# Image units by matrix products under the LSTM: five per image instead of three, with a third PSUM bank

## The reference, cut to what matters

```python
x = x + halo_attention(_gn(x))            # 8x8 blocks, windows of 14x14, 4 heads
x = x + lstm_over_columns(_gn(x))         # 96 time steps, hidden size 128, then a linear layer
x = x + deformable_conv(_gn(x))           # below
x = x + _L3_conv_ref(_gn(x), L3_conv_M)   # an 8x8 block transform on both sides
```

```python
offset = conv2d(x, p_w, p_b, 1, 1)
m = jax.nn.sigmoid(conv2d(x, m_w, m_b, 1, 1))
...
x_off = g_lt[:, None] * gather(qx_lt, qy_lt) + g_rb[:, None] * gather(qx_rb, qy_rb) + g_lb[:, None] * gather(qx_lt, qy_rb) + g_rt[:, None] * gather(qx_rb, qy_lt)
x_off = x_off * jnp.transpose(m, (0, 2, 3, 1))[:, None]
...
return conv2d(x_off, conv_w, None, stride=KS, padding=0)
```

## Time and profile before

| | |
|---|---|
| median of 3 runs | 3619.52 us |
| the profiled execution: time, span | 3624.01 us, 3622.2 us |
| first gather on POOL starts | 519.1 us |
| attention(1), lstm(1), prepare(1) begin | 563.6, 870.7, 1222.9 us |
| attention(2), lstm(2), prepare(2) begin | 1315.1, 1624.6, 1981.7 us |
| attention(3), lstm(3), prepare(3) begin | 2085.3, 2406.3, 2766.8 us |
| transform(0) begins, sampling after transform(1) begins | 2881.1, 2947.1 us |
| last gather starts, transform(3) begins | 3589.65, 3600.6 us |

### The profile page before, as it was taken

One profiled execution on the slowest core, in us unless ns is written; L12 is line 12 of the kernel. 1 busy time (PEld: TensorE's weight loads), 2 busy tenths in 40 slices (PEclk: granted clock), 3 DMA queues, 4 the chain that ended last, 5 costly groups with the idle time before them and its releaser, 6 DMA issues. The chain is left out here.

```text
span 3622.2 us, 59607 instructions
## 1 busy us (share of the span) xinstructions
PE 2785.3 (77%) x21833; PEld 2027.9 (56%) x21833; DVE 2479.2 (68%) x5480; ACT 1263.4 (35%) x3105; POOL 2380.0 (66%) x2445
## 2 busy tenths in 40 slices
PE   6979984885899748867998568668987376889882
PEld 4667763664676526646666346546665254555542
DVE  4754447985777669965777679756777675677763
ACT  4644433542433315523333145324333121222210
POOL 3200026777777777777777777777777777777774
PEclk9999996886899868876999779768999688999995
DMA  6622025764321346636212376543213432222211
GB/s 214 194 60 73 1 71 166 208 174 93 88 60 53 106 145 192 193 82 123 59 53 68 96 216 193 145 94 87 59 54 104 87 94 73 65 63 70 59 53 48
DMA packets 270803, 374.53 MB, mean 103 GB/s; under 512 B 109508, under 2 KB 181336, under 8 KB 269992
## 3 DMA queue, kind: packets, MB, share of 16 engines
q1 hardware_dynamic: 166688, 200.21, 19.2%
q0 software_dynamic: 76896, 157.64, 16.0%
q10 hardware_dynamic: 26928, 12.87, 1.6%
HBM read 270.08 MB, written 99.55 MB: 102 GB/s over the span
## 5 line engine op out<-in xcount | busy, mean ns | idle before, releaser
L769 POOL DMA_INDIRECT got<-sample_table,index x2403 | 2325.2, 968 | 1092.3 <-issue 726.6
L1618 PE MATMUL gates<-cells,row_hat 128*128 128x400 f32 x1782 | 653.3, 513 | 67.8 <-DVE spanned L1153 53.2
L1618 PEld LDWEIGHTS gates<-cells,row_hat 128*128 128x128 f32 x1782 | 332.7, 194 | 309.6 <-issue 84.2
L1175 DVE TENSOR_TENSOR got<-got,bank 128x864 f32<-128x864 f32 x267 | 279.6, 1047 | 242.5 <-DMA got<-sample_table,index 234.3
L852 ACT ACTIVATE pt<-gates 98x512 f32<-98x512 f32 x528 | 288.6, 594 | 325.8 <-PE gates L1726 304.7
L1826 PEld LDWEIGHTS gates<-hist,whh 128*128 128x128 f32 x2280 | 313.5, 205 | 138.7 <-DVE hist L1469 100.8
L1826 PE MATMUL gates<-hist,whh 128*128 128x96 f32 x2280 | 325.9, 290 | 53.8 <-DVE hist L1469 53.1
L1286 DVE TENSOR_REDUCE mx<-gates 128x2 f32<-128x392 f32 x576 | 295.5, 553 | 82.3 <-PE gates L1712 80.9
L1606 PE MATMUL bank<-turned,wout 128*128 128x96 f32 x1728 | 244.9, 304 | 131.5 <-DVE turned L1203 66.1
L1606 PEld LDWEIGHTS bank<-turned,wout 128*128 128x128 f32 x1728 | 239.0, 219 | 156.4 <-DVE turned L1203 110.5
L1712 PE MATMUL gates<-kst,qst 96*128 96x196 bf16 x1152 | 185.2, 278 | 119.7 <-DVE mx L1286 103.1
(11 more groups left out here) (188 smaller groups left out, 4791.6 us busy)
## 6 DMA issues: line engine op xcount, KB each, us to landing
kst<-k_parts SPq DMA_DIRECT2D x96, 441.0 KB
got<-sample_table,index POOLq DMA_INDIRECT x2403
qst<-q_parts SPq DMA_DIRECT2D x96, 288.0 KB
k_parts<-kp SPq DMA_DIRECT2D x24, 882.0 KB
k_parts<-kp SPq DMA_DIRECT2D x24, 588.0 KB
q_parts<-qp SPq DMA_DIRECT2D x24, 576.0 KB
spread<-locations ACTq DMA_DIRECT2D x84, 144.0 KB, 3.9
sample_table<-tab SPq DMA_DIRECT2D x12, 784.0 KB
```

What stands on the lines that cost most here:

```text
L769: pool.indirect_dma_start(out=got[:, g % RING, n, :], out_offset=None, in_=tables[p], in_offset=bass.IndirectOffsetOnAxis(ap=at, axis=0)). ...
L1175: dve.tensor_tensor(corners, corners, w[:, :, 0:3].unsqueeze(3).to_broadcast([P, NTAP, 3, C]), ALU.mult).then_inc(weighted, 1)
L1618: mm = pe.matmul(sums_of(s, h), row_hat[:, 3 * v % HATS + n // TAPS3, t, n % TAPS3, :], cells[:, t, C // 2 * h:C // 2 * (h + 1), :].rearra ...
```

## The change

Five units of each of images 0, 1, 2 (62 to 66) are made by products under the next LSTM instead of three (60 to 62): 45 steps or 270 products in each of lstm(1) to lstm(3), before 27 steps or 162. 27 units are then made by products, and 261 gathered (2349 gathers, before 2403). Nothing changes in which units of image 3 are made by products.

The products start at time step 12 instead of 14 and are spread to step 94. Their sums rotate through three PSUM banks (3, 4, 6). To free bank 3, the output gate moves into bank 1 beside the tanh gate; PE therefore waits in every step for the tanh activation (`g_act`) before the output gate's recurrent product, and the output gate's inputs come first. DVE calls its point ahead of its dense sums, and reads a half in the step in which PE makes it instead of the next. The row positions of the units are turned by one transpose of 36 rows for each unit, copied from up to three banks, and stored by one DMA. `SAMPLES` buffers and `located` share `dense_work`.

The units of each stage change: attention 26, 25, 26 (before 28, 28, 29), with 7, 4, 5 of them in its first six points; LSTM 34, 34, 34 (31, 31, 32); `prepare` 12, 12, 12 (9, 11, 11), of which 7 are gathered (6, 8, 8). 215 units are done by the end of prepare(3), before 210, and 216 by that of transform(1) in both.

```diff
-        stages += [(6 + 3 * NU, ATTENDED[p]), (W, STEPPED[p]), (prep_points(p), PREPARED[p])]
+        stages += [(6, BEGUN[p]), (3 * NU, ATTENDED[p]), (W, STEPPED[p]), (prep_points(p), PREPARED[p])]
...
-ATTENDED = (0, 28, 96, 167)
-STEPPED = (0, 59, 127, 199)
-PREPARED = (0, 68, 138, 210)
-SHARED = (213, 216, 230)
+BEGUN = (0, 7, 76, 148)
+ATTENDED = (0, 26, 97, 169)
+STEPPED = (0, 60, 131, 203)
+PREPARED = (0, 72, 143, 215)
+SHARED = (215, 216, 230)
...
-DENSE_GROUPS = tuple((p, 20) for p in range(LAST)) + ((LAST, 6), (LAST, 11), (LAST, 16), (LAST, 21))
...
+LUNITS = 5
+BATCHES = tuple((p, 62, LUNITS) for p in range(LAST)) + tuple((LAST, first, GUNITS) for first in (18, 33, 48, 63))
...
-FIRST_PIECE = 14
-FIRST_HAT = 8
+FIRST_PIECE = 12
+FIRST_HAT = 6
...
-    n = t - FIRST_PIECE + 1
-    return min(max(4 * (n // 2) + 3 * (n % 2), 0), PIECES * GSTEPS)
+    n, whole = max(t - FIRST_PIECE + 1, 0), W - 1 - FIRST_PIECE
+    return min(PIECES * USTEPS * (8 * (n // 2) + 5 * (n % 2)) // (4 * whole + 1), PIECES * USTEPS)
...
-        sums += [half[0] + 1, half[1] + 1, half[1] + 2]
+        sums += [half[0], half[1], half[1]]
...
-        both_gate = [bank[1][:, 0:2 * W], bank[2][:, 0:2 * W], bank[2][:, 2 * W:4 * W], bank[3][:, 0:2 * W]]
+        both_gate = [bank[1][:, 0:2 * W], bank[2][:, 0:2 * W], bank[2][:, 2 * W:4 * W], bank[1][:, 2 * W:4 * W]]
...
-        step_dense_ps = (bank[4], bank[6])
-        located_ps = [b[0:LOCATIONS, 0:P] for b in bank[1:5]]
+        step_dense_ps = (bank[3], bank[4], bank[6])
+        located_ps = [b[0:LOCATIONS, :] for b in bank[1:4]]
...
-            return (step_dense_ps[h] if s < LSTEPS else dense_ps[s % 2][h])[:, 0:HALF]
+            return (step_dense_ps[(2 * s + h) % 3] if s < LSTEPS else dense_ps[s % 2][h])[:, 0:HALF]
...
-                        act.activation(gc[:, 0, :], both_gate[0][:, h:h + W], ACT.Tanh)
+                        act.activation(gc[:, 0, :], both_gate[0][:, h:h + W], ACT.Tanh).then_inc(g_act, 1)
...
-                    while p > 0 and dense_done < 3 * GSTEPS * p and SUM_AT[dense_done - 3 * GSTEPS * (p - 1)] <= t:
+                    point()
+                    while p > 0 and dense_done < 3 * USTEPS * p and SUM_AT[dense_done - 3 * USTEPS * (p - 1)] <= t:
                         dense_sum(dense_done // 3, dense_done % 3)
                         dense_done += 1
-                    point()
...
-                    wait(pe, dense_read, 2 * (s - (2 if late and s >= LSTEPS + 2 else 1)) + h + 1)
+                    wait(pe, dense_read, 2 * (s - 2) + h + 1 if late else 2 * s + h - 2)
...
-                    for n, g in enumerate(BOTH_GATE_OF):
-                        w = slice(HID * g, HID * (g + 1))
-                        pe.matmul(both_gate[n], wa[:, w], xin, start=(n != 2), stop=False, skip_group_check=True)
+                    for n in (3, 0, 1, 2):
+                        w = slice(HID * BOTH_GATE_OF[n], HID * (BOTH_GATE_OF[n] + 1))
+                        pe.matmul(both_gate[n], wa[:, w], xin, start=(n in (3, 1)), stop=False, skip_group_check=True)
...
                     for n, g in enumerate(BOTH_GATE_OF):
+                        if n == 3:
+                            pe.wait_ge(g_act, W * p + t + 1)
```

More of the change, by code:

```diff
@@ L228, in dense_points @@
     steps, done, last = [LSTEPS] * len(due), LSTEPS, -1
-    for k in (k for p, k in DENSE_GROUPS if p == LAST):
-        usable = [i for i in points if i > last and due[i - 1] < PARTS * (UNITS * LAST + GUNITS * k + 1)]
+    for first in (first for p, first, _ in BATCHES if p == LAST):
+        usable = [i for i in points if i > last and due[i - 1] < PARTS * (UNITS * LAST + first + 1)]
         for m, i in enumerate(usable):
@@ L355, in network @@
             mx1 = sb("mx1", [P, CH, NTAP], where=a2)
[L356 to L359, removed]
+            cell_of = sb("cell", [P, LUNITS, NTAP], where=a2)
+            other_of = sb("other", [P, LUNITS, NTAP], where=a2)
+            inner_of = sb("inner", [P, LUNITS, NTAP], where=a2)
+            cell_rows = sb("cell_rows", [P, max(IMAGE_UNITS), NTAP, CELLS], where=a2)
         with ExitStack() as a3:
@@ L546, in hats_of, with banks_of, banks_upto @@
         def hats_of(d):
-            late = d - LAST
-            return first_hat if late <= 0 else later_hat[:, late - 1]
+            n = BATCHES[d][2]
+            return first_hat[:, 0:n] if d <= LAST else later_hat[:, d - LAST - 1]
         def sums_of(s, h):
-            return (step_dense_ps[h] if s < LSTEPS else dense_ps[s % 2][h])[:, 0:HALF]
+            return (step_dense_ps[(2 * s + h) % 3] if s < LSTEPS else dense_ps[s % 2][h])[:, 0:HALF]
         def groups_of(p):
-            return [d for d, (of, _) in enumerate(DENSE_GROUPS) if of == p]
+            return [d for d, (of, _, _) in enumerate(BATCHES) if of == p]
+        def banks_of(p):
+            return [(first, min(first + 4, IMAGE_UNITS[p])) for first in range(0, IMAGE_UNITS[p], 4)]
+        def banks_upto(p):
+            return sum(len(banks_of(of)) for of in range(p))
         block = ctx.enter_context(nc.Block())
@@ L921, in lstm @@
                 if p > 0:
-                    for v in range(GUNITS * (p - 1), GUNITS * (p - 1) + SPREADS):
+                    for v in range(LUNITS * (p - 1), LUNITS * (p - 1) + SPREADS):
                         load_spread(v)
@@ L995, in prepare @@
                     masks(n)
-                for i, d in enumerate(groups_of(p)):
-                    act.wait_ge(rows_turned, d + 1)
-                    wait(act, dense_summed, GSTEPS * p)
-                    act.activation(located[:, i, :], located_ps[i], ACT.Copy).then_inc(rows_copied, 1)
+                if p > 0:
+                    act.wait_ge(samp_turned, DENSE_UNIT[LUNITS * p - 1] + 1)
+                for i, (first, last) in enumerate(banks_of(p)):
+                    act.wait_ge(rows_turned, banks_upto(p) + i + 1)
+                    act.activation(located[:, P * first:P * last], located_ps[i][:, 0:P * (last - first)], ACT.Copy).then_inc(rows_copied, 1)
             def transform(p):
@@ L1547, in pixel_math @@
                 for d in groups_of(p):
[L1548 removed]
+                    if first <= BATCHES[d][1] < first + N:
                         dense_positions(d)
@@ L1938, in prepare @@
                 combine()
-                wait(pe, dense_read, 2 * GSTEPS * p)
+                wait(pe, dense_read, 2 * USTEPS * p)
                 for i in range(EARLY):
@@ L1951, in prepare @@
                 pe.wait_ge(tab_copied, len(TURNS) * (p + 1))
-                for i, d in enumerate(groups_of(p)):
-                    pe.wait_ge(dense_ready, d + 1)
-                    pe.transpose(located_ps[i], cell_rows[:, i].rearrange("p u n a -> p (u n a)"),
-                                 ident[:, :]).then_inc(rows_turned, 1)
+                pe.wait_ge(dense_ready, groups_of(p)[-1] + 1)
+                for i, (first, last) in enumerate(banks_of(p)):
+                    for u in range(first, last):
+                        mm = pe.transpose(located_ps[i][:, P * (u - first):P * (u - first + 1)], cell_rows[:, u].rearrange("p n a -> p (n a)"),
+                                          ident[:, :])
+                    mm.then_inc(rows_turned, 1)
             def transform(p):
```

88 lines of the change are left out of this document (48 added, 40 removed).

## The result

| | before | after |
|---|---|---|
| median | 3620.26 us (4 runs, 3618.96 to 3622.64) | 3724.28 us (4 runs, 3724.10 to 3726.81) |
| ratio of the times | | 1.0295, 95% interval 1.0282 to 1.0308 |
| span of the profiled execution | 3622.2 us | 3722.3 us |
| lstm(1), (2), (3) | 352.2, 357.1, 360.5 us | 419.5, 424.7, 424.5 us |
| attention(1), (2), (3) | 307.1, 309.5, 321.0 us | 285.5, 282.9, 295.6 us |

A forecast was written before the change was run, and what follows sets the result against it. POOL's gathers set the pace; PE's products would make the LSTMs the bound. Sampling begins at 2947.1 + 220 - 92 - 12 - 17 = 3046 us; plus 5, 54 x 11.25 and 31.6: span 3690, median 3687 us, range 3595 to 3745.

The forecast's parts named there:

- no change: Whole kernel: each LSTM grows by 51 us instead of 73.5, giving 3620 us; chance 0.06.
- the stronger absorption: LSTMs: growth of only 53 to 60 us each, giving 3626 to 3647 us; chance 0.07.
- The first rival: LSTMs: PE has room, growth under about 25 us, POOL stays the pace, 3545 us; chance 0.09.
- DVE and PE hold each other up: LSTMs: same-step reads delay `prod`, `hist` comes late, growth of 95 us, 3751 us; chance 0.14 for over 90 us.
- LSTM: Three LSTMs: each grows by 73.5 us, from a mean of 356.6 to 430; +220 us together.
- The `g_act` wait: PE in each LSTM, ahead of the output gate's product: 4 us, with bounds of nothing and 24 us.
- Bank and reads: LSTMs: third sum bank gains nothing; reads in the same step count nothing, up to 20 us above.
- Attention: Three attentions: gather waits go, -71.2 us, and eight units leave, -21 us; -92 us in the sum.
- Prepare: Prepare stages: gather waits -18.0 us, one gathered unit less -3.4, dense units +2.9, column weights +6.2; together -12 us.
- Transforms: Transforms 0 and 1: 66.0 us with six units, now one unit; -17 us.
- The end: From sampling's start: 5 us to the first free buffer, 54 units of 11.25 us, then 31.6 us.
- Span and median: Whole kernel: span 3690 us; the before kernel's difference between profiled execution and median gives a median of 3687 us.

The follow-up runs named there:

- four units and five in the transforms: Changed kernel with four units per LSTM by products instead of five, and five units instead of one read in transforms 0 and 1: 3596.46 us, ratio 0.9956.
- short reads: Changed kernel with all products, but DVE reading only 25 of 400 columns of the sums except in each LSTM's first step: 3719.05 us, ratio 1.0295.
- two thirds of the products: Changed kernel with two of three row tiles multiplied in each dense step of the LSTMs: 3618.87 us, ratio 1.0003.

## Why the prediction held, and where its terms were off

The mechanism is the one forecast. PE's products set the LSTM, the LSTM becomes longer than its gathers, POOL fills its ring and stops, and 67 us of gathers are bought with more than that. The LSTMs' growth of 64 to 68 us lies in the forecast's band of 60 to 90, and above those of "no change" (51) and of the stronger absorption (53 to 60). The run with four units shows the same account near balance. From one attention to the next, the changed kernel takes 807.8 and 806.4 us and POOL needs 67 units by 11.25, 754; before, 751.5 and 770.2 us against 69 units, 776; with four units and five in the transforms, 769.5 and 776.5 us against 68 units, 765. Of these three only the changed kernel leaves POOL over 50 us an image to stand still. One reading of the forecast was not exact, without consequence: lstm(3) did have a wait of DVE for a gather, of 0.4 us.

The first rival, that PE has room, failed. The Trainium skill (Perfetto Trace Analysis, Identifying the Most-Contended Engine) would judge PE not by its busy time but by its share of peak arithmetic and its weight loads. No view here gives the first, and the forecast named only the second. The weight loads are busy 279 of 424 us in the changed lstm(3), still a third under its length, while the runs with short reads and with fewer products show that PE sets the stage. Here the measurement decides against judging by the weight loads. "DVE and PE hold each other up" failed for five units, by the run with short reads, and is true at two thirds of the products.

The span came out 32 us above its forecast of 3690. By terms:

- **LSTM, +199 us for +220.** Products and convolutions were priced at 75.5 us an LSTM, and PE's busy time grew by 74 to 77. That the two agree is in part chance, as the busy time holds more than the products. Counted from each pass's start to the start of PE's next instruction, or to its own end if that is earlier, the products of lstm(3) took 115 us before and 185 after: 70 for 73.7. The `g_act` wait, priced at 4 us, is the term that was too small. The view of waits shows 0.6 to 1.6 us of it, but the recurrences themselves got longer. In the stretch of the earlier trace rows, the same 656 passes that took 86.4 us before, now after the change and in the run with the gates' old places and no `g_act` wait:

```profile
L1848 PE MATMUL gates<-hist,whh 128*128 128x96 f32 x656 | 95.8, 281 | 1.8 <-ACT gc L955 1.3 <-DVE hist L1489 0.5
```

```profile
L1846 PE MATMUL gates<-hist,whh 128*128 128x96 f32 x656 | 86.7, 276 | 0.0
```

PE's passes overlap in the trace (656 of 281 ns are busy for only 95.8 us), so a fourth product that starts late makes the recurrence longer and leaves no idle time to be listed: 9 us in this stretch. From the start of the pass ahead of it to its own start the fourth product now takes 0.17 us in the median step of lstm(3), before 0.11; that is some 6 of the 9 us, and the rest is open. The arrangement as a whole costs less, some 4 us an LSTM (the run with three units), as other waits go with it. Of the convolutions, priced at 1.8 us in each LSTM, only lstm(1) has one more. The `hist` waits gave 4 to 7 us over a whole LSTM, for 4. And 3 to 6 us came from a wait that I had not looked at, PE's for `row_hat`. A slower stage is not the reason: with three units in the new arrangement, where lstm(3) lasts 361.0 us for 360.5, that wait is 0.6 us already. What in the arrangement removes it is not shown.
- **Bank and reads, nothing for nothing.** The forecast saw nothing to gain because the trace before had no wait for a free bank. With five units and neither of the two edits there is one of 78 us, and the LSTMs are 97 to 102 us longer than the change's. The term came out at nothing because the change brings the remedy along, not for the reason given.
- **Attention, -73.6 us for -92.** This is a step that failed: I took four fifths of the DVE work of the eight units moved out, 21 us, as gain. DVE's busy time did fall, by 28.8 us over the three, and the waits for gathers by 71.2. But DVE's waits for PE rose by some 31 us. Once the waits for gathers are gone, PE ends DVE's waits, and DVE's relief was worth 2 us in sum: attention(1) and (2) fell by 4 us more than their waits for gathers, attention(3) by 6 less. This is read from the waits; no run took DVE's work away there by itself.
- **Prepare, +7 us for -12.** The same step failed here. DVE's work grew by 9 us (priced at 6), the waits for gathers, 18 us, went, and in their place stand three of 3.2 to 3.6 us for PE's convolution (`turned`), which had no such row before, and 6.6 us more for `ot` in prepare(3), 2 us less in prepare(1) and (2). That makes 9 - 18 + 10 + 5, 6 of the 7 us. Prepare(3) after the change, and its `ot` row before:

```profile
DVE raw L1543 <- ACT ot L988: 21.3, 2, 11.0
DVE turned L1223 <- PE bank L1626: 3.6, 1, 3.6
```

```profile
DVE raw L1523 <- ACT ot L971: 14.7, 2, 11.0
```

- **Transforms, -8 us for -17.** Five units fewer gave 1.6 us each, where I had counted DVE's full 3.35: DVE is busy 29 of 66 us there and was not the limit.
- **The end, 8 us.** 55 units were left for 54, as the last of the 216 is read only when sampling begins; POOL went on 2.1 us after it, for 5.
- **Span and median.** I put the median 3 us below the span; it lies 2 us above.

The range held in part by luck, because the errors had both signs: 21 us one way, 54 the other.

## What to carry to other kernels

When work is taken from the engine that sets the pace, compare, for each cycle of the program, what that engine has left to do with how long the cycle is without it: once the second number is larger, each further unit costs nearly its price on the other engine (here 35 us of 37), and the best split lies where the two are equal (here four units; five were not tried with as many units read in the transforms). Before counting a wait that goes as a gain, look for the next wait behind it: in prepare 18 us of waits went and 15 us of others came. A wait among overlapping passes need not show as idle time, so compare the busy time of groups with the same count too. And before a buffer is added to take away a wait, see whether reading it earlier does it alone.

## What the runs showed of the hardware

Little of the products' price was unexpected: a pass of 400 float32 columns takes 0.341 us back to back, and 108 passes more, from four units to five, made an LSTM 35 us longer, 0.32 us each. Not expected was the granted clock's part: it stood at 0.95 and 0.96 in the longer LSTMs, 0.91 and 0.92 before, and at 0.81 to 0.84 in the attentions after the change, 0.78 in attention(1) before. PE's same products in attention were busy 10 to 13 us less. No run here separates that from the order of the work.
